# A 256-column GpSimd clear after every second row scatter

## The chip, the cores and the metric

The kernel runs on 1 core of one Trainium2 chip. The metric is the device time of one execution in microseconds (us). It is compared between the kernel before and the kernel after.

## The reference

The input is `hidden`, 16 sequences of 512 tokens with 256 features. Two layers are computed. The first is a memory layer: keys, values and queries go through a 4-tap causal convolution, per chunk of 128 tokens a gradient of a two-matrix loss updates a state, and the state answers the queries. Its output is normalised, gated and added to the input. The second layer routes each token to one of 8 experts and multiplies its row by that expert's matrix.

```python
x = L0_attn_hidden
x = _layernorm(x + attention(x, ...))                  # memory layer
scores = jnp.einsum('bsh,eh->bse', x, gate_w)
chosen = jnp.argmax(scores, axis=-1)                   # one of 8 experts for each token
expert_out = jnp.einsum('bsh,efh->bsef', x, expert_w)
x = _layernorm(x + x + chosen_expert_out)              # x + ffn(x), where ffn(x) = x + expert output
```

## The kernel before

The 16 sequences are taken in G = 4 groups of NB = 4, and the 512 tokens in NC = 4 chunks of 128, so there are 16 blocks, numbered 0 to f. Each block goes through `project`, `respond`, `learn`, `retrieve` and `epilogue`. Each of these is a generator that yields between steps, and the string `ORDER` says by hand which generator advances next; so the order of instructions on each engine is written out. `Counts.mark` and `Counts.wait` count one semaphore for each engine; TensorE (PE) adds one to its own after the last matmul of a step.

The end of `epilogue` (lines 1029 to 1034) is the first place of the change. GpSimd (POOL) casts four columns of row numbers to integers (`index`, L1029), and then issues four indirect DMAs (L1033), one for each of the block's 4 sequences. Each scatters 128 rows of 1040 bytes to `sorted_rows` in device memory, where each expert has a region. This is a run of four indirect DMAs with nothing between them. What comes next in POOL's queue is an operation of another step, such as `rstd` (L955 to L960) or `ck` (L715).

The second layer works on tiles of 128 sorted rows: 71 tiles in 36 pairs, `experts()` in `ORDER` as `x0`. For pair t, `load` (SyncE, SP) reads the tile numbers from a table into registers and loads the tiles (L1216); `turn` transposes them on PE (L1225) and copies them on ScalarE (ACT, L1228); `multiply` multiplies by the expert's matrix (L1248) and takes the statistics on VectorE (DVE, L1252 and L1257); `scale` computes the scale (ACT L1267, DVE L1269 and L1271); `send` writes the scaled rows (ACT L1282) and scatters each tile to its tokens in `out` with an indirect DMA on POOL (L1287). The lags are 0, 0, 2, 1 and 2 pairs. Six buffers hold loaded tiles (`LOADS`) and four hold output tiles (`ROWS_OUT`). In `send`, ACT waits until the scatter of pair t-4 has landed; in `multiply`, DVE waits for that of t-6. Tables of tile numbers are built after blocks b, d and f (`TABLES`), so that most of the second layer runs beside the last blocks of the first, and 24 of the 72 tile places come after the last block.

`send` is the second place of the change. Where pairs follow each other without other work for POOL, its queue holds nothing but indirect DMAs.

Of the kernel before, what the change touches and what calls it, by code (L numbers as in the profile page):

```python
# [27 lines left out]
P = 128  # L28
B = 16
S = 512  # L30
H = 256
# [37 lines left out]
class Counts:  # L69
# [9 lines left out]
    def mark(self, e, name, instruction):  # L79
        instruction.then_inc(self.sem[e], 1)  # L80
        self.count[e] += 1
        self.at[name] = (e, self.count[e])

    def wait(self, e, *names):

        need = {}
        for name in names:
            if int(name.rsplit(".", 1)[1]) >= 0:
                who, n = self.at[name]
                need[who] = max(need.get(who, n), n)  # L90
        for who, n in need.items():
            if self.reached[e, who] < n:
                self.engines[e].wait_ge(self.sem[who], n)
                self.reached[e, who] = n
# [54 lines left out]
def build(nc, dram):  # L149
    out = dram["out"]  # L150
    with ExitStack() as ctx:
# [193 lines left out]
        nc.vector.wait_ge(s_prep, n_bias)  # L345

        layers(nc, ctx, sb, sem, dict(locals()))


def layers(nc, ctx, sb, sem, v):  # L350
# [12 lines left out]
    pe, act, dve, pool, sp = nc.tensor, nc.scalar, nc.vector, nc.gpsimd, nc.sync  # L363
# [3 lines left out]
    def two(name, shape, dt=F32):  # L367
        return [sb(f"{name}{i}", shape, dt) for i in range(2)]
# [65 lines left out]
    where_f = sb("where_f", [P, NB])  # L434
    index = two("index", [P, NB], I32)
    s_scatter = [sem(f"s_scatter{i}") for i in range(2)]

    pro = Slots("pro", banks[0:3], NC * G * 9 + NC * G // 2)
    lrn = Slots("lrn", banks[3:4], NC * G * 4)
# [471 lines left out]
    def epilogue(c, g):  # L911
# [120 lines left out]
        for b in range(NB):  # L1032
            pool.indirect_dma_start(sorted_rows[:, :], bass.IndirectOffsetOnAxis(index[i2][:, b:b + 1], 0), R[:, b, :], None,  # L1033
                                    bounds_check=NE * REGION - 1, oob_is_err=False).then_inc(s_scatter[i2], 16)
        yield

    s_blank = sem("s_blank")
# [144 lines left out]
    def tiles_of(t):  # L1182

        return 1 if t == PAIRS - 1 else 2
# [5 lines left out]
    def moved(t):  # L1190

        return 32 * (t // LOADS) + 16 * tiles_of(t)
# [80 lines left out]
    def send(t):  # L1273

        o = t % ROWS_OUT
        key, both = product[t]
        if t >= ROWS_OUT:
            act.wait_ge(s_out[(t - ROWS_OUT) % LOADS], moved(t - ROWS_OUT))
        wait("act", f"x_shift.{t}")
        for i in range(tiles_of(t)):  # L1280
            mark("act", f"x_os{i}.{t}" if i < tiles_of(t) - 1 else f"x_os.{t}",
                 act.activation(os_[o][:, i, :], both[:, i, :], ACT.Identity, bias=rs[o][:, 2, i:i + 1], scale=rs[o][:, 1, i:i + 1]))  # L1282
        late.freed_by(key, f"x_os.{t}")
        for i in range(tiles_of(t)):
            wait("pool", f"x_os{i}.{t}" if i < tiles_of(t) - 1 else f"x_os.{t}", f"x_tok.{t}")
            M.apart("pool")
            pool.indirect_dma_start(out[:, :], bass.IndirectOffsetOnAxis(xs_token[t % LOADS][:, i:i + 1], 0), os_[o][:, i, :], None,  # L1287
                                    bounds_check=TOK - 1, oob_is_err=False).then_inc(s_out[t % LOADS], 16)

    def experts():  # L1290

        for t in range(PAIRS + 2):
            for stage, lag in ((load, 0), (turn, 0), (scale, 2), (multiply, 1), (send, 2)):
                if 0 <= t - lag < PAIRS:
                    stage(t - lag)
                    yield
# [3 lines left out]
    for letter, stage in dict(p=project, s=respond, l=learn, r=retrieve, e=epilogue).items():  # L1300
        steps.update({f"{letter}{n:x}": stage(n // G, n % G) for n in range(NC * G)})
# [74 lines left out]
```

## Time and profile before

| What | Value |
|---|---|
| median of 3 runs | 544.11 us (542.71 to 547.35) |
| profiled execution, first to last instruction | 578.0 us |
| the profiled execution's time with what lies around it | not given; its span alone is 578.0 us |
| indirect DMAs | 64 of L1033, 71 of L1287 |
| mean granted TensorE clock | 0.910 |

The span is one execution with the hardware profiler on. The runs are timed without it. In a row of the profile, a time in brackets with an arrow is the engine's idle time just before the instruction and the instruction that ended it; "remote" stands where no instruction in the records fits, and "issue" where the engine waited for nothing that the records show.

### The profile page before, as it was taken

To read this page: it belongs to the slowest core of one execution; us is meant where nothing else is said; L and a number is where in the kernel's file an instruction comes from. 1 tells how busy PE (TensorE), PEld (TensorE's weight loads), DVE (VectorE), ACT (ScalarE), POOL (GpSimd) and SP (SyncE) were. 2 spreads that over 40 slices of the span, in tenths; PEclk is the share of its full clock that TensorE was granted. 3 is DMA by queue.
4 is the path that set the end of the run, shared out by engine and by line. 5 is a ranking of instruction groups with operands and counts; after the bars stand their busy time and mean duration, and the time that the engine had idled before them with its cause. 6 is when DMAs were issued, how large, how long until landed. Compare 5 with 4: busy or idle time off the path is not lost.

```text
span 578.0 us, 11149 instructions
## 1 busy us (share of the span) xinstructions
PE 458.5 (79%) x3502; PEld 347.1 (60%) x3502; DVE 376.7 (65%) x1123; ACT 309.7 (54%) x779; POOL 326.8 (57%) x451
## 2 busy tenths in 40 slices
PE   4589889999888998888998898766858774855773
PEld 2356656777665877667675775555646553644662
DVE  3365886898795868769789696777644543333433
ACT  1254375566575485665738656464656553314544
POOL 2004535446748686685757657672477666445466
PEclk9797999999998999998999999885887987768788
DMA  8412352345553536445263545474364644425431
GB/s 228 130 74 61 107 124 71 120 129 101 158 130 96 161 85 164 95 141 135 79 176 74 157 110 151 134 231 110 93 178 133 177 140 137 131 91 161 130 120 43
DMA packets 61354, 73.21 MB, mean 127 GB/s; under 512 B 17293, under 2 KB 48206, under 8 KB 61296
## 3 DMA queue, kind: packets, MB, share of 16 engines
q1 hardware_dynamic: 50624, 46.12, 28.5%
q0 software_dynamic: 8848, 25.44, 16.6%
q10 hardware_dynamic: 1824, 0.93, 0.6%
q8 instruction: 29, 0.48, 0.4%
q14 instruction: 29, 0.24, 0.2%
HBM read 44.19 MB, written 19.22 MB: 110 GB/s over the span
## 4 chain that ended last, share of the span: by engine, by line
PE 41%; DVE 20%; ACT 11%; issue 10%; POOL 8%; another core or an unknown queue 5%; DMA 3%; SPq 1%; ACTq 0%; POOLq 0%; DVEq 0%
DVE kq_in L559 8%; PE bank L518 6%; PE bank L1248 5%; PE bank L605 4%; POOL sorted_rows L1033 3%; PE bank L536 3%; ACT rows L966 2%; PE bank L920 2%; PE both L1248 2%; ACT os L1282 2%; PE bank L686 2%; DVE gt L609 1%; PE both L886 1%; PE bank L1225 1%
## 5 line engine op out<-in xcount | busy, mean ns | idle before, releaser
L1287 POOL DMA_INDIRECT out<-os,xs_token x71 | 70.1, 988 | 46.0 <-ACT os L1282 26.4
L1033 POOL DMA_INDIRECT sorted_rows<-rows,index x64 | 68.7, 1074 | 30.0 <-issue 16.6
L1248 PE MATMUL bank<-shared,front 128*128 x212 | 60.6, 435 | 27.3 <-ACT rs L1267 8.5
L518 PE MATMUL bank<-front 128*64 128x256 f32 x512 | 64.8, 408 | 13.3 <-DMA bias_t<-in_bias_t 7.7
L559 DVE SCALAR_TENSOR_TENSOR kq_in<-shared,conv_w,kq_in 128x256 f32<-128x256 f32 x144 | 69.0, 536 | 9.5 <-ACT kq_in L553 9.3
L605 PE MATMUL bank<-front 128*128 128x256 f32 x256 | 63.1, 396 | 4.8 <-DVE bias_g L324 4.8
L1248 PEld LDWEIGHTS bank<-shared,front 128*128 128x128 f32 x212 | 43.9, 219 | 36.5 <-issue 30.3
L518 PEld LDWEIGHTS bank<-front 128*64 128x64 f32 x512 | 38.8, 148 | 34.4 <-issue 10.8
L605 PEld LDWEIGHTS bank<-front 128*128 128x128 f32 x256 | 48.2, 196 | 12.7 <-issue 6.6
L937 DVE SCALAR_TENSOR_TENSOR y<-bank,rms,gt 128x256 f32<-128x256 f32 x64 | 26.5, 476 | 17.1 <-POOL rms L933 10.2
L1252 DVE BATCH_NORM_STATS2 st<-bank 128x6 f32<-128x256 f32 x53 | 20.2, 421 | 26.3 <-remote 11.9
L927 ACT ACTIVATE junk<-bank 128x256 f32<-128x256 f32 x64 | 24.6, 384 | 22.7 <-PE bank L920 10.2
L966 ACT ACTIVATE rows<-y,rstd 128x256 f32<-128x256 f32 x64 | 33.2, 595 | 5.6 <-POOL rstd L960 3.3
L1228 ACT ACTIVATE front<-bank 128x512 f32<-128x512 f32 x28 | 16.7, 596 | 35.7 <-remote 24.8
L1282 ACT ACTIVATE os<-bank,rs 128x256 f32<-128x256 f32 x53 | 27.0, 560 | 15.2 <-DVE rs L1271 12.2
L536 PE MATMUL bank<-front 128*128 128x512 f32 x64 | 31.6, 617 | 0.0
L609 DVE TENSOR_TENSOR gt<-bank,bias_g 128x512 f32<-128x512 f32 x32 | 21.2, 680 | 10.8 <-PE bank L605 10.7
L1248 PE MATMUL both<-shared,front 128*128 x72 | 22.9, 474 | 5.7 <-ACT front L1228 4.7
L850 POOL TENSOR_TENSOR ab_h<-hq,carry 128x512 f32<-128x512 f32 x13 | 17.4, 1340 | 14.8 <-DMA hq<-hq 14.8
L553 ACT ACTIVATE kq_in<-shared,conv_b,conv_w 128x256 f32<-128x256 f32 x48 | 25.3, 595 | 0.8 <-PE bank L686 0.8
L948 DVE BATCH_NORM_STATS2 stats<-y 128x6 f32<-128x256 f32 x64 | 22.4, 411 | 3.5 <-DMA y<-in_hidden 3.5
L793 DVE TENSOR_REDUCE norms<-sq 128x16 f32<-128x1024 f32 x16 | 19.5, 1216 | 7.3 <-ACT sq L790 5.6
(212 smaller groups left out, 1185.3 us busy)
## 6 DMA issues: line engine op xcount, KB each, us to landing
front<-sorted_rows SPq DMA_DIRECT2D x71, 130.0 KB
front<-in_hidden_t SPq DMA_DIRECT2D x16, 512.0 KB
decay<-gate_clear SPq DMA_DIRECT2D x16, 512.0 KB
y<-in_hidden POOLq DMA_DIRECT2D x16, 512.0 KB
q<-kq_in SPq DMA_DIRECT2D x64, 64.0 KB, 2.1
carry<-carry_rows SPq DMA_DIRECT2D x32, 128.0 KB, 2.8
hq<-hq SPq DMA_DIRECT2D x64, 64.0 KB
shared<-in_w_expert SPq DMA_DIRECT2D x2, 1024.0 KB
```

What stands on the lines that cost most here:

```text
L518: ins = pe.matmul(halves[half(side), kind, :, :], w[:, k, kind * D:(kind + 1) * D], pairs[:, k, side, :, :], start=k == 0, stop=k == KH - 1)
L536: ins = pe.matmul(bank[:, :], w_ae[:, k, :], xt[:, k, :], start=k == 0, stop=k == KH - 1)
L553: act.activation(kq_in[i2][:, kind, :, :], raw[g][:, kind, :, 0:P], ACT.Identity, bias=conv_b[:, kind:kind + 1], scale=conv_w[:, kind, 0:1]))
L559: dve.scalar_tensor_tensor(dst, raw[g][:, kind, :, tap:tap + P], conv_w[:, kind, tap:tap + 1], dst, ALU.mult, ALU.add))
L605: ins = pe.matmul(bank[:, (b % 2) * H:(b % 2 + 1) * H], xt[:, k, b * P:(b + 1) * P], w_g[:, k, :], start=k == 0, stop=k == KH - 1)
L609: mark("dve", n(f"gt{two_of}"), dve.tensor_tensor(gt[g][:, 2 * two_of:2 * two_of + 2, :], bank[:, :].rearrange("p (b f) -> p b f", b=2), s ...
L937: mark("dve", n(f"gated{b}"), dve.scalar_tensor_tensor(Y[:, b, :], wo[b], rms[:, 1, b:b + 1], gt[g][:, b, 0:H], ALU.mult, ALU.mult))
L966: act.activation(R[:, b, 0:H], Y[:, b, :], ACT.Identity, bias=rstd[:, 2, b:b + 1], scale=rstd[:, 1, b:b + 1])
L1033: pool.indirect_dma_start(sorted_rows[:, :], bass.IndirectOffsetOnAxis(index[i2][:, b:b + 1], 0), R[:, b, :], None, bounds_check=NE * REGI ...
L1248: ins = pe.matmul(both[:, i, :], xs_t[t % TURNED][:, i, k, :], w_expert[:, k, bass.ds(expert, 1), :], start=k == 0, stop=k == KH - 1)
L1282: act.activation(os_[o][:, i, :], both[:, i, :], ACT.Identity, bias=rs[o][:, 2, i:i + 1], scale=rs[o][:, 1, i:i + 1]))
L1287: pool.indirect_dma_start(out[:, :], bass.IndirectOffsetOnAxis(xs_token[t % LOADS][:, i:i + 1], 0), os_[o][:, i, :], None, bounds_check=TO ...
```

## The change

A tile `spare` of 128 x 256 fp32 is added, with a semaphore `s_apart`. `keep_apart()` clears it on GpSimd. Before each clear GpSimd waits for the clear before it. It is called after the second and the fourth scatter of each block, 32 times, and at the end of `send`, 36 times: 68 clears in all. Nothing reads the tile.

```diff
+    spare = sb("spare", [P, H])
+    s_apart = sem("s_apart")
+    cleared = [0]
+
+    def keep_apart():
+
+        if cleared[0]:
+            pool.wait_ge(s_apart, cleared[0])
+        pool.memset(spare[:, :], 0.0).then_inc(s_apart, 1)
+        cleared[0] += 1
...
         for b in range(NB):
             pool.indirect_dma_start(sorted_rows[:, :], bass.IndirectOffsetOnAxis(index[i2][:, b:b + 1], 0), R[:, b, :], None,
                                     bounds_check=NE * REGION - 1, oob_is_err=False).then_inc(s_scatter[i2], 16)
+            if b % 2:
+                keep_apart()
         yield
...
             pool.indirect_dma_start(out[:, :], bass.IndirectOffsetOnAxis(xs_token[t % LOADS][:, i:i + 1], 0), os_[o][:, i, :], None,
                                     bounds_check=TOK - 1, oob_is_err=False).then_inc(s_out[t % LOADS], 16)
+        keep_apart()
```

## Rows read from the trace of the kernel before

**Rows 1.** The page's first part: busy time, share of the span, instructions.

```profile
PE 458.5 (79%) x3502; PEld 347.1 (60%) x3502; DVE 376.7 (65%) x1123; ACT 309.7 (54%) x779; POOL 326.8 (57%) x451
```

**Rows 2.** The chain of work that ended last, shares by engine, then by line.

```profile
PE 41%; DVE 20%; ACT 11%; issue 10%; POOL 8%; another core or an unknown queue 5%; DMA 3%; SPq 1%; ACTq 0%; POOLq 0%; DVEq 0%
DVE kq_in L559 8%; PE bank L518 6%; PE bank L1248 5%; PE bank L605 4%; POOL sorted_rows L1033 3%; PE bank L536 3%; ACT rows L966 2%; PE bank L920 2%; PE both L1248 2%; ACT os L1282 2%; PE bank L686 2%; DVE gt L609 1%; PE both L886 1%; PE bank L1225 1%
```

**Rows 3.** POOL's row scatters over the span: busy us, mean ns, idle before.

```profile
L1033 POOL DMA_INDIRECT sorted_rows<-rows,index x64 | 68.7, 1074 | 30.0 <-issue 16.6 <-POOL index L1029 12.8 <-ACT sq L783 0.3
```

**Rows 4.** Busy time by stretch: PE, PEld, DVE, ACT, POOL, clock, DMA share, GB/s.

```profile
200.00:300.00 100.00, 90.44 (x812) 69.15 (x810) 78.22 (x196) 61.40 (x162) 69.05 (x98) 0.98 0.49 126
...
425.00:503.00 78.00, 53.31 (x314) 41.74 (x315) 32.96 (x173) 35.87 (x88) 48.07 (x59) 0.80 0.50 149
503.00:578.00 75.00, 43.66 (x183) 35.25 (x181) 26.71 (x136) 30.08 (x69) 39.99 (x42) 0.80 0.35 110
```

**Rows 5.** POOL's timeline, 171 to 182 us: start us, us, instruction, idle before.

```profile
173.32 1.12 POOL L1033 DMA_INDIRECT sorted_rows<-rows,index  x1 [0.91 <-POOL index L1029]
...
177.33 0.97 POOL L1033 DMA_INDIRECT sorted_rows<-rows,index  x1 [0.30 <-issue]
178.38 0.24 POOL L955 TENSOR_SCALAR rstd<-mv 128x4 f32<-128x4 f32 x1
```

**Rows 6.** Timelines of PE, ACT and DVE, 171 to 182 us.

```profile
177.54 0.42 PE L644 MATMUL bank<-ident,kq_in 128*128 128x128 f32 x2
...
179.28 0.60 ACT L895 ACTIVATE state<-both 128x512 f32<-128x512 f32 x1 [4.11 <-PE bank L644]
...
179.34 0.42 DVE L787 SCALAR_TENSOR_TENSOR grad<-ds,bank 128x256 f32<-128x256 f32 x1 [3.63 <-PE bank L644]
```

**Rows 7.** POOL's timeline, 471 to 480 us: two pairs with one operation between.

```profile
473.85 0.97 POOL L1287 DMA_INDIRECT out<-os,xs_token  x1 [0.30 <-PE both L1248]
474.84 0.26 POOL L1021 TENSOR_TENSOR routed<-routed,onehot 128x32 bf16<-128x32 bf16 x1
475.27 0.99 POOL L1287 DMA_INDIRECT out<-os,xs_token  x1 [0.17 <-issue]
476.57 0.98 POOL L1287 DMA_INDIRECT out<-os,xs_token  x1 [0.30 <-issue]
477.55 0.20 POOL L1029 CAST index<-where_f 128x4 int32<-128x4 f32 x1
```

**Rows 8.** Timelines of PE and ACT, 471 to 480 us.

```profile
474.29 0.66 PE L1225 MATMUL bank<-ident,front 128*128 128x128 f32 x4
...
478.35 0.60 ACT L1228 ACTIVATE front<-bank 128x512 f32<-128x512 f32 x1 [1.94 <-remote]
```

**Rows 9.** SP's timeline: loads of tiles at the start and beside twelve scatters.

```profile
399.94 10.34 SPq L1216 DMA_DIRECT2D front<-sorted_rows  x12
...
504.05 7.90 SPq L1216 DMA_DIRECT2D front<-sorted_rows  x4
```

**Rows 10.** Waits, 503 to 578 us: total us, times, longest.

```profile
ACT front L1228 <- remote: 25.5, 5, 7.1
```

**Rows 11.** POOL's groups from 503 to 578 us.

```profile
L1287 POOL DMA_INDIRECT out<-os,xs_token x41 | 39.9, 973 | 33.9 <-ACT os L1282 21.6 <-issue 10.1 <-DVE st L1252 1.8
```

**Rows 12.** ACT's timeline, 519 to 529 us: the beat of `send` in two pairs.

```profile
522.47 1.02 ACT L1282 ACTIVATE os<-bank,rs 128x256 f32<-128x256 f32 x2 [0.49 <-DVE rs L1271]
...
524.65 1.02 ACT L1282 ACTIVATE os<-both,rs 128x256 f32<-128x256 f32 x2 [0.49 <-DVE rs L1271]
```

**Rows 13.** POOL's groups with their shapes: clears, and selects of two widths.

```profile
L290 POOL TENSOR_SCALAR_AFFINE_SELECT ident_nb<-ident_nb 128x512 f32<-128x512 f32 x1 | 0.6, 630 | 0.0
...
L290 POOL TENSOR_SCALAR_AFFINE_SELECT ident<-ident 128x128 f32<-128x128 f32 x1 | 0.3, 282 | 7.4 <-DVE coef L278 7.4
...
L1039 POOL MEMSET rows<- 128x16 f32 x2 | 0.2, 111 | 0.1
...
L1371 POOL MEMSET const-float32-0.0<- 128x1 f32 x1 | 0.1, 98 | 0.3 <-issue 0.3
```

## The prediction

> **What bounds the kernel now.** I read the page's busy shares first, then the chain, then the stretches, and then the timelines around the indirect DMAs, since the change only adds work there. TensorE is busy for 79% of the span and is the largest part of the chain, 41%; GpSimd is busy for 57% and has 8% of it [rows 1, 2]. From 200 to 300 us TensorE is busy for 90 of 100 us. In the last stretch, 503 to 578 us, no engine is: TensorE 43.7 of 75 us, GpSimd 40.0 [rows 4]. So the first part is bound by TensorE with its partners, and the last is bound by waits.
>
> What these waits are is the point of this case. A run of four scatters lasts from 173.32 to 178.30 us [rows 5]. TensorE ends its step at 177.96, but ScalarE, which names that step as its releaser, has been idle for 4.11 us and starts at 179.28, and VectorE after 3.63 us at 179.34 [rows 6]. That is 1.3 us after the matmul's end and 1.0 us after the run's end. All three engines stand still at the end of the run. It looks as if TensorE's signals are held while indirect DMAs follow each other. I call this a hold. SyncE is slowed as well: 12 loads take 10.34 us where GpSimd is quiet, 0.86 us each, and 4 loads take 7.90 us beside the run of twelve, 2.0 us each [rows 9]. In the last stretch ScalarE waits five times, for 25.5 us, before its copy of the transposed tile [rows 10]. So the holds cost the profiled execution perhaps 20 us in that stretch (the 25.5 less some 5 us for which it would have waited anyway), and if each of 14 earlier runs stops the engines for 1 us, 14 us more: 34 us.
>
> The profiled span is 578.0 us and the median of the runs is 544.1, so the timed runs are 33.9 us shorter. The 34 us of holds are about this size, and I see nothing else in the trace that would shrink so much without the profiler. I therefore take it that the holds belong mostly to the profiled execution, and that a change which acts on them hardly acts on the timed runs. This is a choice from one coincidence of sizes, and the chances below say how far I trust it.
>
> **The change part by part.** First the price of a clear. The clears shown are 98 ns for 1 column and 111 ns for 16, or 0.87 ns a column, which gives 98 + 255 x 0.87 = 320 ns at 256 columns. The selects are 282 ns at 128 columns and 630 at 512, or 0.91 ns a column, which gives 282 + 128 x 0.91 = 398 ns [rows 13]. I take 0.34 us, nearer to the clears, since the operation is a clear. The ends are 0.29 us (a cheaper column than any shown) and 0.40 us.
>
> Then what it adds to GpSimd's queue. Between two scatters GpSimd idles for 0.30 us, but after another operation only for 0.17 us, because the next DMA is prepared meanwhile: with an operation of 0.26 us between, the starts are 475.27 - 473.85 = 1.42 us apart, and without, 1.30 us [rows 7]. So an operation between scatters costs its length less 0.13 us: 0.34 - 0.13 = 0.21 us, between 0.14 and 0.27. A clear that is followed by another operation, as after a block's fourth scatter, costs its whole 0.34 us, because such an operation starts some 0.1 us after the scatter as it is [rows 5]. The wait for the clear before costs nothing: that clear ended two scatters earlier, 2.5 us. Behind the wait stands GpSimd's own queue, but it never waits. The tile is read by nobody, so no other engine waits for it.
>
> Where it lies. Three stretches:
>
> Up to block b, 12 blocks: 12 clears inside runs and 12 after them, 12 x 0.21 + 12 x 0.34 = 6.6 us on GpSimd. What follows in its queue (`rstd`, `ck`) is work for which others wait, and the scatters themselves are on the chain, 3% of it or some 17 us of their 68.7 us [rows 2, 3]. So not a quarter, but with what stands behind them perhaps 40% of the delay reaches the end: 2.6 us. The cover of the rest is TensorE, busy for 90% [rows 4]; if that cover were gone it would be all 6.6 us.
>
> From 418 to 503 us: 8 clears for the last four blocks and 15 in `send`, for the 30 outputs that precede 503 us (of all 71, 41 come later [rows 11]): 23 x 0.21 = 4.8 us. GpSimd is busy for 48 of 78 us in most of this stretch, and its waits between scatters come on top [rows 4]. I put half on the path: 2.4 us.
>
> After 503 us: 41 scatters and 20 clears between them. The step of `send` repeats on ScalarE every 524.65 - 522.47 = 2.18 us when nothing is held [rows 12]. GpSimd needs 2 x (0.97 + 0.30) = 2.54 us for the pair's two scatters [rows 5, 11]. So without holds GpSimd is the slowest member here: 41 scatters are 52 us of queue, and each clear lengthens it by 0.21 us. With them, 20 x 0.21 = 4.2 us. In the profile GpSimd idles for 21.6 us waiting for ScalarE [rows 11], but that is what the holds make. I take 60% of it, 2.5 us, because the tables and the first loads also leave gaps. If everything counts it is 4.2 us; with the profile's gaps it would be near 1 us, the clears in the last burst.
>
> The sum is 2.6 + 2.4 + 2.5 = 7.5 us. Against the profiled span, 578.0 + 7.5 = 585.5 us if the holds stay as they are; against the median 544.1 + 7.5 = 551.6 us, or 1.4% slower. All of it on the path with a clear of 0.40 us is 24 x 0.34 + 43 x 0.27, near 20 us; nothing on the path is 0. A likelier spread is 3 to 13 us.
>
> Does the clear end a hold, where there is one? The trace has the very pattern: two scatters, an operation of 0.26 us, two scatters. TensorE ends its transposes at 474.95 us, but ScalarE's copy of them starts at 478.35, 0.8 us after the fourth scatter's end at 477.55 [rows 7, 8]. The break of 475.27 - 474.82 = 0.45 us did not let the signal through. With the clear the break is 0.34 + 0.17 = 0.51 us, hardly longer. After the run of rows 5 the signal took 1.0 us to come. So by these rows a break must be some 0.8 to 1.0 us, and the clear is too short by half.
>
> A rule of the Trainium skill bears on whether the profiler makes the holds. "NOTIFIC — the notification-queue block", section 10, says that emitting a record costs the engine no cycles; by that the holds would be in the timed runs too. Its section 7.1 says that the block's internal queue pushes back on the engines when it fills, rather than lose a record; by that the profiler can stall them. The trace shows a stall, but no row says which of the two it is. Another rule, "Perfetto Trace Analysis", section "GPSIMD Engine Instruction", has it that GpSimd's spans are unreliable and that spacing of starts is to be used; the 1.42 us against 1.30 follows it, and by the span of 0.26 us alone each clear would cost 0.34 in place of 0.21 us and the sum would be nearer 11 us.
>
> **The rivals.**
>
> Holds are real and the change shortens them. For it: the stall is seen on four engines at once, and the coincidence with 34 us proves nothing. Against it: the break of 0.45 us that let nothing through. If each of 14 front runs loses 1 us of standstill and the last stretch half of its 20 us, the gain is 24 us, less the 7.5 us of clears: 528 us, 3% faster. A milder case, half of that gain, gives 540 us. The clear must open the hold within 0.5 us for this. Chance 0.17, both together.
>
> The clears are hidden. GpSimd is busy for 57% of the span and only 8% of the chain [rows 1, 2]; if the tail in the timed runs has its gaps as in the profile, about 1 us is lost there and 1 or 2 us before: 547 us, no measurable change. It decides if ScalarE or TensorE sets the pace of the last stretch. Chance 0.30.
>
> The clears cost more than their length, the other end: GpSimd is the pace everywhere after 418 us, and the delays of its small operations in blocks 0 to b reach the end in most blocks: 6.6 + 4.8 + 4.2 = 15.6 us, 560 us. It begins to decide where GpSimd's pair of 2.54 us exceeds what every other engine needs, which is so after 503 us already. Chance 0.10.
>
> The change could fail to do what it says where `send` for two pairs is apart anyway; there runs already have two members, and its clears then fall into idle time. This is part of the hidden case.
>
> **How the numbers follow.** The forecast, 551.5 us, has 0.43, with its own range of 548 to 556. Hidden has 0.30, costly 0.10 and shorter holds 0.17. The range of 80% reaches down to 538 us, which takes in the milder half of the gain, and up to 558 us. What a measurement of this kernel can tell from no change is about 1%, 5.4 us: below 538.7 is faster, above 549.5 slower. Faster gets 0.14 (most of the holds' case); slower gets the costly case and most of the forecast's own range, 0.10 + 0.38 = 0.48, and a little of nothing else; the rest, 0.38, is within 1%.
>
> **What the profile of the changed kernel would show.** 68 clears of 0.29 to 0.40 us, each between scatters that start some 1.5 us apart, with 0.17 us idle after the clear. If the break is too short, ScalarE and VectorE still wait for 3 to 4 us in the runs of the front blocks, and ScalarE for about 25 us after 503 us. If those waits are gone from the profile while the timed median is not lower, the holds were the profiler's. If both fall, the real-hold rival was right and I was wrong in the step where I gave the 34 us to the profiler. If the clears are far longer than 0.4 us, their price was wrong. In the last stretch GpSimd's queue should be as long as before plus some 4 us, and the idle time for ScalarE shows whether it is the pace.

## The result, and the profile after

| | before | after |
|---|---|---|
| median | 544.11 us (542.71 to 547.35) | 558.04 us (556.36 to 561.39) |
| first to last instruction, profiled execution | 578.0 us | 557.5 us |
| that execution's time | not given | 558.7 us |

The ratio after to before is 1.0242, with a 95% interval of 1.0167 to 1.0317. So the change costs 13.9 us, between 9 and 17 us, from four runs of each kernel. The forecast was 551.5 us. The direction is right, but half of the cost is missing, and 558.04 lies at the very edge of the range that ended at 558. Medians, here and below, are over all runs of a kernel, and ratios are over its fast runs alone (those within 1.5% of its fastest), so that the two do not always divide out.

The two profiles seem to say the opposite: the span falls by 20.5 us while the time rises by 14. That contradiction has to be solved before a row of one trace is set beside a row of the other. One premise stated ahead of the prediction does not help here: that the runs are timed without the profiler. On record the profiled execution is one of the timed runs, and every run lists its own span and granted clock. So no number here compares an execution with recording against one without.

From the page of the changed kernel come the busy shares, the chain's shares, and two rows of POOL's groups:

```profile
PE 446.2 (80%) x3502; PEld 337.7 (61%) x3502; DVE 379.3 (68%) x1123; ACT 308.8 (55%) x779; POOL 348.1 (62%) x519
...
DVE 24%; PE 24%; POOL 21%; ACT 12%; issue 11%; DMA 8%; SPq 1%; POOLq 0%; ACTq 0%; DVEq 0%
...
L1044 POOL DMA_INDIRECT sorted_rows<-rows,index x64 | 69.0, 1079 | 27.8 <-issue 13.8
L1300 POOL DMA_INDIRECT out<-os,xs_token x71 | 70.1, 988 | 17.8 <-issue 12.2
```

GpSimd has 21% of the chain in place of 8%, TensorE 24% in place of 41% [rows 1, 2]. "Another core or an unknown queue", 5% before, is gone. The scatters themselves have not changed: 69.0 and 70.1 us.

POOL's timeline of the run of scatters that answers to rows 5, now with its two clears:

```profile
175.95 1.11 POOL L1044 DMA_INDIRECT sorted_rows<-rows,index  x1 [0.91 <-POOL index L1040]
177.36 1.00 POOL L1044 DMA_INDIRECT sorted_rows<-rows,index  x1 [0.30 <-issue]
178.33 0.36 POOL L445 MEMSET spare<- 128x256 f32 x1
178.86 0.97 POOL L1044 DMA_INDIRECT sorted_rows<-rows,index  x1 [0.17 <-issue]
180.14 1.31 POOL L1044 DMA_INDIRECT sorted_rows<-rows,index  x1 [0.30 <-issue]
181.43 0.35 POOL L445 MEMSET spare<- 128x256 f32 x1
181.87 0.24 POOL L966 TENSOR_SCALAR rstd<-mv 128x4 f32<-128x4 f32 x1
```

ACT's and DVE's timelines in the same stretch, the two instructions that answer to rows 6:

```profile
178.61 0.60 ACT L906 ACTIVATE state<-both 128x512 f32<-128x512 f32 x1 [0.82 <-PE both L899]
...
179.11 0.42 DVE L798 SCALAR_TENSOR_TENSOR grad<-ds,bank 128x256 f32<-128x256 f32 x1 [0.78 <-PE bank L786]
```

The product that the copy of `state` waits for is TensorE's last `ch` matmul of the block, L888 before and L899 after. PE's timelines, before and then after:

```profile
175.56 0.39 PE L888 MATMUL both<-grad_w,ch 128*128 128x64 f32 x2
```
```profile
178.19 0.39 PE L899 MATMUL both<-grad_w,ch 128*128 128x64 f32 x2
```

Before, ScalarE waited for 4.11 us and VectorE for 3.63, and both started after the run's end [rows 6]; ScalarE started 3.33 us after its product had ended at 175.95. Now they wait for 0.8 us and start in the run's middle, ScalarE 0.03 us after its product. The copy of `state` begins during the first clear, which invites the reading that the clears opened the holds. The experiments show that they did not.

In the last part ScalarE waits for something else than in rows 10. These are its waits from 499 to 557.5 us:

```profile
ACT os L1295 <- DMA out<-os,xs_token: 14.0, 12, 1.8
ACT os L1295 <- DVE xs_token L1274: 4.3, 1, 4.3
```

Not one "remote" wait is left. ScalarE waits for a scatter to land so that it gets its output buffer back, which means it is ahead of GpSimd. And this is POOL from 499 to 557.5 us:

```profile
L1300 POOL DMA_INDIRECT out<-os,xs_token x41 | 39.8, 972 | 9.6 <-issue 6.0 <-ACT rs L1280 1.4 <-ACT os L1295 0.8
L445 POOL MEMSET spare<- 128x256 f32 x22 | 7.4, 338 | 0.0
```

The idle time before 41 scatters is 9.6 us, 0.23 us each: the gap of 0.30 or 0.17 us between instructions and nothing more. Before, it was 33.9 us, 21.6 of it for ScalarE [rows 11]. GpSimd hardly waits for data here; it is the pace.

### The profile page after: what moved, and what is told of

It reads as the page before. It is cut to its first block, busy times and chain, and to the rows that moved or that the text cites. A ratio compares the mean times of both kernels' runs of the same rounds, so it can differ in the third digit from the quotient of the medians.

```text
span 557.5 us, 11217 instructions
## 1 busy us (share of the span) xinstructions
PE 446.2 (80%) x3502; PEld 337.7 (61%) x3502; DVE 379.3 (68%) x1123; ACT 308.8 (55%) x779; POOL 348.1 (62%) x519
## 3 DMA queue, kind: packets, MB, share of 16 engines
q1 hardware_dynamic: 50624, 46.12, 29.8%
## 4 chain that ended last, share of the span: by engine, by line
DVE 24%; PE 24%; POOL 21%; ACT 12%; issue 11%; DMA 8%; SPq 1%; POOLq 0%; ACTq 0%; DVEq 0%
DVE kq_in L570 9%; POOL sorted_rows L1044 6%; PE bank L529 5%; POOL out L1300 4%; ACT rows L977 4%; DMA y<-in_hidden 3%; PE bank L1261 3%; DMA out<-os,xs_token 3%; PE bank L547 2%; PE bank L616 2%; ACT os L1295 2%; POOL rstd L969 2%; POOL spare L445 2%; DVE gt L620 2%; DVE grad_w L826 2%
## 5 line engine op out<-in xcount | busy, mean ns | idle before, releaser
L1300 POOL DMA_INDIRECT out<-os,xs_token x71 | 70.1, 988 | 17.8 <-issue 12.2
L570 DVE SCALAR_TENSOR_TENSOR kq_in<-shared,conv_w,kq_in 128x256 f32<-128x256 f32 x144 | 70.4, 546 | 11.4 <-ACT kq_in L564 11.2
L529 PE MATMUL bank<-front 128*64 128x256 f32 x512 | 63.1, 402 | 9.6 <-DMA bias_t<-in_bias_t 9.5
L1261 PE MATMUL bank<-shared,front 128*128 x212 | 55.0, 405 | 8.5 <-ACT rs L1280 4.6
L616 PEld LDWEIGHTS bank<-front 128*128 128x128 f32 x256 | 48.3, 197 | 12.7 <-issue 6.6
L529 PEld LDWEIGHTS bank<-front 128*64 128x64 f32 x512 | 37.3, 145 | 30.5 <-DMA bias_t<-in_bias_t 9.5
L1261 PEld LDWEIGHTS bank<-shared,front 128*128 128x128 f32 x212 | 40.4, 201 | 16.3 <-issue 11.5
L984 PE MATMUL bank<-ident,rows 128*128 128x128 f32 x128 | 20.1, 309 | 11.1 <-DVE y L948 10.6
L620 DVE TENSOR_TENSOR gt<-bank,bias_g 128x512 f32<-128x512 f32 x32 | 21.2, 682 | 11.1 <-PE bank L616 11.0
L804 DVE TENSOR_REDUCE norms<-sq 128x16 f32<-128x1024 f32 x16 | 19.5, 1216 | 11.1 <-ACT sq L801 11.1
L861 POOL TENSOR_TENSOR ab_h<-hq,carry 128x512 f32<-128x512 f32 x13 | 17.3, 1327 | 14.9 <-DMA hq<-hq 14.8
L808 POOL TENSOR_TENSOR small<-norms 128x8 f32<-128x8 f32 x16 | 4.6, 288 | 34.3 <-DVE norms L804 34.3
L984 PEld LDWEIGHTS bank<-ident,rows 128*128 128x128 f32 x128 | 16.7, 160 | 14.1 <-DVE y L948 11.9
```

What stands on the lines that cost most here:

```text
L529: ins = pe.matmul(halves[half(side), kind, :, :], w[:, k, kind * D:(kind + 1) * D], pairs[:, k, side, :, :], start=k == 0, stop=k == KH - 1)
L570: dve.scalar_tensor_tensor(dst, raw[g][:, kind, :, tap:tap + P], conv_w[:, kind, tap:tap + 1], dst, ALU.mult, ALU.add))
L616: ins = pe.matmul(bank[:, (b % 2) * H:(b % 2 + 1) * H], xt[:, k, b * P:(b + 1) * P], w_g[:, k, :], start=k == 0, stop=k == KH - 1)
L620: mark("dve", n(f"gt{two_of}"), dve.tensor_tensor(gt[g][:, 2 * two_of:2 * two_of + 2, :], bank[:, :].rearrange("p (b f) -> p b f", b=2), s ...
L984: ins = pe.transpose(bank[:, b * P:(b + 1) * P], R[:, b, k * P:(k + 1) * P], ident[:, :])
L1261: ins = pe.matmul(both[:, i, :], xs_t[t % TURNED][:, i, k, :], w_expert[:, k, bass.ds(expert, 1), :], start=k == 0, stop=k == KH - 1)
```

## The experiments

Every run's first-to-last span was recorded beside its time, and the two differ by 1.2 us or so on every run. A late signal is counted where TensorE's counter moves more than 0.8 us after the last matmul of its step; several steps that wait for one movement count once, with the longest delay. The traces miss some records of such movements, so counts and sums of late signals are rough, to 15 or 20%.

**Parts and lengths, first chip.** Rows only: `keep_apart()` is taken out of `send`. Send only: it is taken out after the row scatters. One column is the first diff, double the second:

```diff
-        pool.memset(spare[:, :], 0.0).then_inc(s_apart, 1)
+        pool.memset(spare[:, 0:1], 0.0).then_inc(s_apart, 1)
```
```diff
-    spare = sb("spare", [P, H])
+    spare = sb("spare", [P, 2 * H])
```

> The clears of send are left out; the 32 clears after the row scatters stay. Theory Q (the cost is GpSimd's queue time, and nearly all of it reaches the end): 16 clears inside runs at 0.18 to 0.21 us and 16 after them at 0.34 us are 8.5 us, so 551 to 553 us. Theory S (the shares that I forecast, 40% in front and 50% later): 12 x 0.55 x 0.4 + 4 x 0.55 x 0.5 = 3.7 us, 548 us, and the rest of the measured 14 us is then in send or is no queue time. Theory T (all of the cost lies in the last part, the front is hidden behind TensorE): 545 us. In the profiled execution the holds of ScalarE and VectorE are gone from the front blocks and are still there in send, where the runs are unbroken: its span is some 10 to 20 us longer than the timed runs.

> The clears after the row scatters are left out; the 36 of send stay. Theory Q: 36 x 0.18 to 0.21 = 6.5 to 7.5 us, 551 us. Theory S: 15 x 0.21 x 0.5 + 20 x 0.21 x 0.6 = 4.1 us, 548 us. Theory T: 558 us. In the profiled execution the holds stay in the row scatters of the front blocks and are gone after 503 us: the span is some 10 to 15 us longer than the timed runs.

> All 68 clears, each of 1 column in place of 256, about 0.10 us in place of 0.34. Theory Q: inside a run the clear is shorter than the 0.13 us that it hides, so it costs nothing; after a run it costs 16 x 0.10 = 1.6 us: 544 to 546 us. A rival, that what costs is the operation itself (its semaphore, or the order that it breaks) and not its length, gives 556 to 558 us. Profiled execution: if a hold ends as soon as any operation stands between two indirect DMAs, the span is within 2 us of the timed runs; if it takes a break of half a microsecond, the span is still 20 us or more above them.

> All 68 clears, each of 512 columns, about 0.59 us in place of 0.34 (98 ns + 511 columns at the 0.96 ns that the step from 1 to 256 columns gives). Theory Q: 68 x 0.25 = 17 us more than the changed kernel, 575 us. Theory S (44% of the queue time reaches the end): 7.5 us more, 565 us. The rival of e3 (a price for each operation): 558 to 560 us. The profiled span is within 2 us of the timed runs.

On this chip the kernel before took 579.86 us, 36 us more than in the result. The ratios to it were 1.0006 (0.9964 to 1.0048) for rows only, 0.9945 (0.9903 to 0.9988) for send only, 1.0109 (1.0044 to 1.0174) for one column and 0.9991 (0.9943 to 1.0038) for double. So they say nothing on the price in the result. All four traces are full of late signals. In double's run of scatters from 174.90 us, POOL's timeline leaves 0.70 us between the end of the second scatter and the start of the third. ACT's copy still starts only at the run's end. But the product for it, last on PE's line below, ended at 178.64, after the break. So a hold of 1.63 us stands here beside the third and fourth scatter, and this run does not say whether the break would have ended an older one:

```profile
176.32 1.01 POOL L1044 DMA_INDIRECT sorted_rows<-rows,index  x1 [0.30 <-issue]
177.28 0.58 POOL L445 MEMSET spare<- 128x512 f32 x1
178.03 0.98 POOL L1044 DMA_INDIRECT sorted_rows<-rows,index  x1 [0.17 <-issue]
179.31 0.98 POOL L1044 DMA_INDIRECT sorted_rows<-rows,index  x1 [0.30 <-issue]
```
```profile
178.25 0.39 PE L899 MATMUL both<-grad_w,ch 128*128 128x64 f32 x2
```
```profile
180.27 0.60 ACT L906 ACTIVATE state<-both 128x512 f32<-128x512 f32 x1 [2.42 <-PE both L915]
```

Both theories on holds fall: holds are there with the clears in place, and the profiled executions (576.25, 569.12, 582.35 and 575.07 us) are not longer than the other runs of the same kernels. What was left that had changed was the chip, with the host and the session that come with it.

**The two kernels again, second chip.** Both unchanged.

> The kernel before, unchanged, with a profile on the same chip as its timed runs. Theory C (whether signals are held beside indirect DMAs is a property of the chip or the session that runs the kernel, since the first four experiments ran on a chip where the kernel before took 579.9 us and all their profiles show holds): the profiled time and the timed runs agree within 1%, either both near 544 us with no holds in the trace, or both near 580 us with TensorE's signals late at 25 or more places. The rival, my step that the profiler makes the holds: timed runs near 544 us and a profiled execution near 578.

> The changed kernel, unchanged. Theory C: where the kernel before takes 544 us, this takes 558 and its trace has no holds, so that the clears did not remove them; where the kernel before takes 580 us, holds are in this kernel's trace too, and the time lies between the ratios of the 1-column and the 512-column clears on such a chip (1.011 and 0.999), 574 to 584 us. The rival, that a clear of 0.34 us ends the holds: 558 us and no holds even where the kernel before takes 580 us, 4% faster.

The kernel before took 579.65 us here, and 576.5 in its profiled execution. The changed kernel took 575.62 us, a ratio of 0.9971 (0.9934 to 1.0007): no difference. The same code as in the result has here some 30 late signals, 70 to 90 us in all, where the first trace of it has 2, 4 us in all. ACT and DVE beside the run of scatters that starts at 175.10 us, with the same two clears in it:

```profile
179.68 0.60 ACT L906 ACTIVATE state<-both 128x512 f32<-128x512 f32 x1 [2.73 <-PE bank L639]
...
180.41 0.42 DVE L798 SCALAR_TENSOR_TENSOR grad<-ds,bank 128x256 f32<-128x256 f32 x1 [2.93 <-PE bank L639]
```

And in its last part, 501 to 574 us, POOL's scatters and ACT's longest wait:

```profile
L1300 POOL DMA_INDIRECT out<-os,xs_token x41 | 39.9, 972 | 24.0 <-ACT os L1295 11.5 <-issue 9.1 <-DVE rs L1282 2.5
...
ACT front L1241 <- remote: 19.3, 3, 10.7
```

These are rows 10 and 11 again, with the clears in place. So theory C holds: whether TensorE's signals are held beside indirect DMAs goes with the chip, or with the host or session that comes with it, not with the clears, and not with which execution is profiled. I call the chips "held" and "clean". The profile of before, 578.0 us, is that of a held chip, while the result's runs and the trace of after are of a clean one. The traces bear this out without any time: that of before has 8,026 records of semaphore updates, the eight others from held chips 8,279 to 8,558, and the five from clean chips 11,424 to 11,508, the trace of after among them.

**Scatters of `send` as plain DMAs, a clean chip.** SyncE issues them; this leaves out that rows go to their tokens.

```diff
-            wait("pool", f"x_os{i}.{t}" if i < tiles_of(t) - 1 else f"x_os.{t}", f"x_tok.{t}")
-            M.apart("pool")
-            pool.indirect_dma_start(out[:, :], bass.IndirectOffsetOnAxis(xs_token[t % LOADS][:, i:i + 1], 0), os_[o][:, i, :], None,
-                                    bounds_check=TOK - 1, oob_is_err=False).then_inc(s_out[t % LOADS], 16)
+            wait("sp", f"x_os{i}.{t}" if i < tiles_of(t) - 1 else f"x_os.{t}", f"x_tok.{t}")
+            place = (2 * t + i) % (TOK // P) * P
+            sp.dma_start(out[place:place + P, :], os_[o][:, i, :]).then_inc(s_out[t % LOADS], 16)
```

> The kernel before, with the 71 scatters of send replaced by plain DMAs of the same tiles to fixed rows of the output, issued by SyncE: this leaves out that each row goes to its own token, and takes 71 indirect DMAs from GpSimd. If the holds come from indirect DMAs, on a chip where the kernel before takes 580 us: no signal of TensorE is late beside send any more, the last part is paced by ScalarE's 2.18 us a pair, and the time is 540 to 550 us; if they come from elsewhere, 575 us. On a chip where the kernel before takes 544 us: theory Q (GpSimd's 2.54 us a pair is the pace after the last row scatter) gives 530 to 537 us; the hidden rival (GpSimd is not the pace) gives 543 to 545 us.

The kernel before took 549.26 us, this one 694.02. As a test of the pace it failed, and as it fell on a clean chip it also left untested whether the holds of a held chip come from the indirect DMAs: SyncE waits 163.6 us in all for ScalarE's `os`, with the loads of the first layer queued behind it. But up to block b it is the kernel before, on a clean chip, without a single late signal, and I use it for that.

**Clears in the last part alone, third held chip.** Twenty clears of 512 columns in `send`, none before pair 16 and none after the row scatters; and the kernel before, for its trace. Against the kernel before, with `spare` and `keep_apart()` added:

```diff
+    spare = sb("spare", [P, 2 * H])
...
+        if t >= 16:
+            keep_apart()
```

> Clears only in send and only from pair 16 on (20 clears, after the last row scatter), each of 512 columns, 0.56 us; the row scatters and the first 16 pairs are as in the kernel before. On a chip where the kernel before takes 544 to 549 us: theory Q (GpSimd's queue is the pace after the last row scatter, all of its time counts) gives 19 x (0.56 - 0.13) = 8.2 us more, a ratio of 1.015; the shares that I forecast (60%) give 4.9 us, 1.009; the hidden rival gives 1.000. On a chip where it takes 580 us: TensorE's late signals set the pace of that part and the clears fall beside them, ratio 0.99 to 1.00 as for the changed send alone (0.9945).

> The kernel before, unchanged, for its trace. On a chip where it takes 544 to 549 us: no late signals; GpSimd's scatters stand back to back from the last row scatter to the end (pairs every 2.55 us), the last row scatter of block b starts near 384 us and that of block f near 486 to 489, and the time after it is 55 to 58 us. Theory S would show GpSimd waiting for ScalarE in a third or more of that part. On a chip where it takes 580 us it repeats the traces that are there.

The kernel before took 576.04 us and 574.95. The 20 clears of 0.55 us gave 0.9946 (0.9894 to 0.9998): where signals are held, GpSimd has room, and the clears cost nothing. The second kernel repeats the trace of before and tells nothing new.

The first trace shows what a break does to a hold, in the timelines of PE, ACT and POOL:

```profile
500.59 0.60 PE L1236 MATMUL both<-ident,front 128*128 128x128 f32 x4
```
```profile
511.72 0.60 ACT L1239 ACTIVATE front<-both 128x512 f32<-128x512 f32 x1 [10.15 <-remote]
```
```profile
505.65 0.97 POOL L1298 DMA_INDIRECT out<-os,xs_token  x1 [0.30 <-issue]
506.61 0.55 POOL L445 MEMSET spare<- 128x512 f32 x1
507.33 0.97 POOL L1298 DMA_INDIRECT out<-os,xs_token  x1 [0.17 <-issue]
508.61 0.97 POOL L1298 DMA_INDIRECT out<-os,xs_token  x1 [0.30 <-issue]
509.57 0.55 POOL L445 MEMSET spare<- 128x512 f32 x1
510.28 0.97 POOL L1298 DMA_INDIRECT out<-os,xs_token  x1 [0.17 <-issue]
```

TensorE ends its transposes at 501.19 us. ScalarE is idle from 501.57 and starts the copy of them 10.5 us after their end. In between GpSimd makes two breaks of 0.7 us, from 506.62 and from 509.58. Neither let the signal through.

**Rows only, on a clean chip.**

> The 32 clears after the row scatters without those of send, a second time. On a chip where the kernel before takes 544 to 549 us: theory Q gives 8.5 us at most (16 x 0.18 + 16 x 0.34), of which 4.5 up to block b, as the traces of the changed kernel and of the plain-output one put it, and 1 to 2 after it: a ratio of 1.010 to 1.016; its last part has no clears, and GpSimd's scatters there stand back to back if GpSimd is the pace of the kernel before. The rival, that all 14 us come from send: 1.000. On a chip where it takes 580 us: 1.000 as the first time.

The kernel before took 546.5 us; the ratio is 1.0113 (1.0053 to 1.0173), 6.2 us, in the range that theory Q gave. Its last part has no clears, so it is the last part of the kernel before on a clean chip. POOL from 498 to 552.7 us, then the timeline's second and last of the 41 scatters:

```profile
L1300 POOL DMA_INDIRECT out<-os,xs_token x41 | 39.9, 973 | 12.4 <-issue 6.7 <-ACT os L1295 1.8 <-ACT front L1241 1.4
...
500.76 0.98 POOL L1300 DMA_INDIRECT out<-os,xs_token  x1 [0.30 <-DVE leap L1127]
...
550.61 0.97 POOL L1300 DMA_INDIRECT out<-os,xs_token  x1 [0.30 <-issue]
```

12.4 us before 41 scatters is 0.30 us each, and 550.61 - 500.76 = 49.85 us for 39 of them is 1.278 each. For 50 us no other engine makes GpSimd wait beyond this gap. The busy times from 498 to 552.7 us, in the columns of rows 4, show who is beside it:

```profile
498.00:552.70 54.70, 35.68 (x183) 29.11 (x181) 26.59 (x134) 28.15 (x67) 41.20 (x43) 0.91 0.50 153
```

GpSimd's 41.2 us and the 12.7 us of gaps fill 53.9 of 54.7 us; TensorE needs 35.7 and ScalarE 28.2.

**Send only and double, on a clean chip.**

> The 36 clears of send without those after the row scatters, a second time. On a chip where the kernel before takes 544 to 549 us: theory Q (GpSimd's queue is the pace from the first send to the end) gives 35 x 0.18 = 6.3 us, a ratio of 1.011 to 1.013; the shares that I forecast give 3.5 us, 1.006. The last row scatter of block b starts near 384 us as without clears. On a chip where it takes 580 us: the ratio of the first time, 0.9945, again below 1 if clears in send shorten TensorE's late signals there, 1.00 if that was chance.

> All 68 clears of 512 columns, 0.56 us, a second time. On a chip where the kernel before takes 544 to 549 us: theory Q gives 52 x (0.56 - 0.16) + 16 x 0.56 = 29.8 us, times the share that the 256-column clears gave (14 of 14.7 us): 28 us, a ratio of 1.05; if half of each clear is covered, 14 us, 1.03. On a chip where it takes 580 us: 0.999 as the first time, with late signals in the trace again.

The kernel before took 543.58 us. Double gave 1.0505 (1.0449 to 1.0561), 28.1 us, where theory Q had said 28. Send only gave 1.0204 (1.0151 to 1.0257), 11.1 us, more than the 6.3 that I had expected; its lowest run, the profiled one, took 550.14 us, 6.6 above the median of before. Double's POOL timeline in the last part:

```profile
546.06 0.98 POOL L1300 DMA_INDIRECT out<-os,xs_token  x1 [0.16 <-ACT rs L1280]
547.34 0.97 POOL L1300 DMA_INDIRECT out<-os,xs_token  x1 [0.30 <-issue]
548.31 0.55 POOL L445 MEMSET spare<- 128x512 f32 x1
549.02 0.97 POOL L1300 DMA_INDIRECT out<-os,xs_token  x1 [0.16 <-ACT rs L1280]
```

The pair repeats every 549.02 - 546.06 = 2.96 us. All the clean traces side by side, in us from the start, each the start of an instruction on POOL's timeline:

| clean chips | first scatter of block 0 | first scatter of block b | first of the last 41 outputs | last output | a pair |
|---|---|---|---|---|---|
| plain output (no clears in front) | 145.42 | 383.64 | | | |
| send only | 145.81 | 384.16 | 491.96 | 546.82 | 2.74 |
| rows only | 148.49 | 390.53 | 499.48 | 550.61 | 2.56 |
| the changed kernel | 147.20 | 388.16 | 500.57 | 555.38 | 2.74 |
| double | 145.79 | 398.57 | 513.52 | 572.67 | 2.96 |

A pair is the difference of the two columns before it, divided by 20. Each clear lengthens it by 0.18 us with 256 columns and by 0.40 with 512. These are the clear's 0.34 and 0.55 us, less 0.13 or 0.14 for the shorter gap and up to 0.03 for its overlap with the end of the scatter. The first column shows how far two traces can lie apart before a single clear has run: 3 us.

## Why the prediction was right in sign and half in size

**The price of a clear: right.** 342 ns, forecast 0.34 us; inside a run 0.18 us, forecast 0.21. A row of the Trainium skill stood beside it, "Perfetto Trace Analysis", section "GPSIMD Engine Instruction": go by the spacing of starts. The clean traces agree: by the spans alone each clear inside a run would cost 0.34 us, and by the starts it costs 0.18. The reason that the prediction gave for the shorter gap, that the next DMA is prepared meanwhile, is shown by no run; the gaps of 0.30 and 0.17 us are.

**The shares that reach the end: wrong, and this is the step that failed.** I put "perhaps 40%" for blocks 0 to b, "half on the path" to 503 us and "60%" after it. With the measured prices GpSimd's whole bill is 16 x 0.18 + 16 x 0.34 = 8.3 us for the rows and 35 x 0.18 = 6.3 us for `send`, together 14.6 us; the measured cost is 13.9 us. With clears of 512 columns the cost is 28.1 us of a bill of 29.8. Nearly everything reaches the end. That holds for the sum; where along the way each part does is shown less well.

After the row scatters of block f it is shown directly. The part between the first and the last of the 41 outputs takes 51.1 us without clears (rows only) and 54.8 with them: 3.7 us, all of 20 x 0.18. I had seen that GpSimd is "the slowest member here" by 2.54 against 2.18 us, and then took 60% "because the tables and the first loads also leave gaps". They leave none. The gaps that I saw were those of a held chip.

In the front, the eleven blocks ahead of block b's scatters carry 11 x (0.18 + 0.34) = 5.7 us of clears. Block b comes 4.0 to 4.5 us later (388.16 against 384.16 and 383.64), but the changed kernel's first scatter, before any clear, is late already. From the first scatter of block 0 to that of block b it takes 240.96 us, rows only 242.04, and the two without clears 238.35 and 238.22: 2.6 to 3.8 us more, 46 to 67% of the bill. On the held chips the changed kernel takes 244.65 us for this way and the profile before 239.65, which is 5.0 us or 88%. Double, on the clean chip, takes 252.78, which is 14.5 us for a bill of 11 x (0.40 + 0.56) = 10.6. So the share of 40% was too low by all of these pairs, but in the lowest by little, and single traces do not fix it. TensorE's 90 of 100 busy us [rows 4] were little cover. A reason would be that `rstd`, `ck` and the scatters themselves stand on the way from one block to the next; that is argued, not shown. A busy share close to one doesn't say that the work which feeds it is hidden.

The middle part, from block b to the first of the last 41 outputs, has no clean trace without clears. What is left for it is 13.9 - 3.2 - 3.7 = 7.0 us, with 3.2 as the mean of 2.6 and 3.8 in front, against a bill there of 14.6 - 5.7 - 3.7 = 5.2 us. It takes 112.41 us in the changed kernel and 107.80 in send only, which lacks the clears of the last five blocks: 4.6 us for a bill of 5 x 0.52 = 2.6. This part shows no cover either, though its size is only argued from differences of single traces.

**"A choice from one coincidence of sizes": the wrong cause, with the right consequence.** I took the 33.9 us between profile and median for "holds" that "belong mostly to the profiled execution". In every session the profiled execution is within 1% of the median of its kernel's runs: 576.5 with a median of 581.71 on a held chip, 558.7 with 558.04 on a clean one. The holds go with the chip: medians of before of 576 to 580 us on three held chips, 543.6 to 549.3 us in the result and on two clean ones. That they hardly act on the runs of the result was right, because those ran on a clean chip. The rule that I set against it, from the Trainium skill, "NOTIFIC — the notification-queue block", section 10, is that a record costs the engine nothing; section 7.1 has it that a full internal queue pushes back on the engines. No run here decides between the two, since every run lists a granted clock and none is known to be without recording. That recording itself makes the holds, on the held chips only, is a rival that stands untested.

I also misread the size of one hold. I took ScalarE's copy of `state` to be 1.3 us late, after the step that the row names (L644). It needs the product of L888, which ended at 175.95, so its signal was 3.3 us late. In the trace of before, TensorE's counter does not move once from there to 179.26 us and then six times in 0.27 us, one for each step that had ended meanwhile. The row names the step that happened to come out last.

The size was a coincidence as well. I counted 14 us of holds in the front. But block b comes at 384.71 us on the held chip and at 383.64 on the clean one (where the plain output changes nothing ahead of it), or 239.65 and 238.22 us after the first scatter, so the front loses about 1 us, and nearly all of the 34 us is lost after it, where the loads, transposes and products of a pair follow each other with nothing else to do.

**"The clear is too short by half": right as far as it goes.** Holds go on across breaks of 0.49 and of 0.71 us. The pair of rows on which the step rested (474.95 and 478.35 us [rows 8]) is weaker than it looks, since TensorE ended 0.13 us into the break. Breaks may shorten some holds: TensorE's signals are late by some 70 us in all where 256 or 512 columns are cleared after the row scatters, and by 72 to 80 in the three traces of before, which is within the roughness of the count. The whole change shows no gain from it in time. My test for it was faulty: I wrote that if the waits were gone from the profile and the median not lower, "the holds were the profiler's". Exactly that came about, for a reason that was in none of my cases: the two profiles were taken on different chips.

**The rivals.** "Costly", 560 us, with a chance of 0.10, was the mechanism: GpSimd is the pace after 418 us, and its delays in front reach the end. "Hidden", 547 us, describes the held chips, where the change measures 0.9971. "Holds are real and the change shortens them" is half true: they are real on such chips, where clears in `send` alone measure 0.5% faster (0.9945 and 0.9946, with intervals that barely leave out 1), but the whole change gains nothing that can be measured.

**Left open.** Why send only costs 11.1 us on the clean chip (8.2 to 14.0) where its bill is 6.3, so that the two parts sum to 17.3 us and the whole is 13.9: the intervals overlap, and its profiled execution fits the bill, but its other runs don't. What makes a chip hold signals, the recording included; whether indirect DMAs are the cause or only beside it; and whether the gain of 0.5% there is real and comes from shorter holds. No version here beats both kernels on both kinds of chip.

## What to carry to other kernels

Before a trace is used to say which engine sets the pace, compare its span with the timed runs. If they are 6% apart, as here, the trace may be of other conditions, and its waits need not be those of the runs. Then the pace has to be computed from what doesn't change between conditions, the durations and gaps of each engine for one step (here 2.56 us on GpSimd against 2.18 on ScalarE), and the engine that comes out slowest gets the whole cost of what is added to it there, as it did here after block f, not a share.

A small operation on an engine with a busy share of about 60% (57% before) can cost nearly its whole queue time, here 13.9 us of 14.6.

## What the hardware showed that I had not expected

One and the same kernel has two times by chip: 579.86, 579.65 and 576.04 us on three chips, 549.26 and later 543.58 on a fourth, 546.5 on a fifth. On the first kind TensorE's signals come up to 13 us late beside indirect DMAs: in the one-column trace the transposes end at 504.39 us and ScalarE's copy starts at 517.16. They come out in bursts, such as six in 0.27 us. On the second kind, all traces together have about four late ones, each under 2 us. TensorE's mean granted clock is 2% lower on the held kind (0.911 and 0.933 for the changed kernel), but up to block b the kernel takes only 1 us longer there, so the clock alone does not explain the 34 us. In the last part it is 0.80 in the trace of before [rows 4] and 0.91 in that of rows only; TensorE, which idles more there when its signals are held, is the pace in neither, since ScalarE's step still comes every 2.18 us on the held chip where nothing is held [rows 12]. A scatter's duration is the same (972 ns in both). A trace of a held chip also has a quarter fewer records of semaphore updates, which may be a sign of the cause or only of the same load on the recording; no run here tells.

A clear of 1 column in all 68 places made the kernel 1.1% slower on a held chip, while clears of 256 and 512 columns made no difference there (0.9971, 0.9991). So the time is not a smooth function of what is added; no run tells why.
